# Rows of the first chunk transposed by a diagonal of inverse deviations, first-layer weights loaded and rounded by blocks

## What is computed

```
xn = layernorm(x)                      # (x - mean) / sqrt(var + 1e-5), per row of 256
D = fractal_dimension(xn)              # one scalar from the first 1024 numbers of xn
x1 = ifft(fft(xn) * wave_filter(D)).real
corrected = golay_correct(sigmoid(x1 @ W_el + b_el) > 0.5)    # 24 bits a token
attn = x1 + corrected @ W_le + b_le
ffn = gelu(xn @ w1 + b1) @ w2 + b2     # 256 -> 1024 -> 256
out = x + attn + ffn
```

## Time and profile before

| | |
|---|---|
| median of 3 runs | 407.12 us (407.1 to 407.69) |
| the profiled execution: its own time | 407.3 us |
| its span, first to last instruction | 405.5 us |
| PE busy | 400.7 us, 99% |
| DVE, ACT, POOL busy | 298.7 (74%), 223.3 (55%), 87.2 us (21%) |
| granted TensorE clock, mean | 1.000 |
| DMA | 35.75 MB, mean 88 GB/s |

### The profile page before, as it was taken

How to read it: one execution, slowest core, us unless ns; L and a number is a source line. 1 busy time by engine, 2 the same in 40 slices (tenths; PEclk the granted TensorE clock), 3 DMA queues, 4 the chain that set the end, 5 groups by cost and what they waited for, 6 DMA issues and landing times.

```text
span 405.5 us, 5548 instructions
## 1 busy us (share of the span) xinstructions
PE 400.7 (99%) x1774; PEld 329.1 (81%) x1774; DVE 298.7 (74%) x512; ACT 223.3 (55%) x333; POOL 87.2 (21%) x102
## 2 busy tenths in 40 slices
PE   8999999999999999999999999999999999999997
PEld 3888888888888888888888888888888888888886
DVE  5879985878658795677957788476974868757656
ACT  3967556557354664537545474554736556365561
POOL 3142421313003131121313013131121312113000
PEclk9999999999999999999999999999999999999999
DMA  6554333213333213333123332023333031111011
GB/s 187 218 158 156 104 103 106 63 42 104 103 104 98 44 65 103 104 103 97 46 64 104 103 104 90 26 91 103 104 103 78 40 89 53 54 52 52 2 52 52
DMA packets 15307, 35.75 MB, mean 88 GB/s; under 512 B 5440, under 2 KB 6592, under 8 KB 15296
## 3 DMA queue, kind: packets, MB, share of 16 engines
q1 hardware_dynamic: 15152, 35.49, 27.4%
q10 hardware_dynamic: 144, 0.13, 0.1%
HBM read 27.17 MB, written 8.45 MB: 88 GB/s over the span
## 4 chain that ended last, share of the span: by engine, by line
PE 97%; DMA 1%; DVE 1%; POOL 0%; SPq 0%; issue 0%
PE p_h L964 43%; PE p_f L982 28%; PE p_f L987 14%; PE p_s L1030 5%; PE p_l L1017 4%; PE p_s L1038 2%; DMA x_sb<-x 1%; PE p_f L997 0%; SPq L248 0%; DVE stats L830 0%; POOL row_nums L361 0%; DVE rows_sb L817 0%; PE p_g L1006 0%; PE p_l L1006 0%; PE p_s L1139 0%
## 5 line engine op out<-in xcount | busy, mean ns | idle before, releaser
L446 ACT ACTIVATE h<-p_h,small_sb 128x512 f32<-128x512 f32 x128 | 88.2, 689 | 139.4 <-PE p_h L964 138.9
L633 DVE TENSOR_TENSOR h_lo<-h,h_hi 128x512 fp32r<-128x512 f32 x128 | 102.9, 804 | 69.2 <-ACT h_hi L454 69.2
L982 PE MATMUL p_f<-h_hi,w_hi 128*128 128x512 f32 x252 | 98.3, 390 | 0.0
L982 PE MATMUL p_f<-h_hi,w_lo 128*128 128x512 f32 x252 | 98.1, 389 | 0.0
L369 POOL TENSOR_TENSOR uv<-xn 128x512 f32<-128x512 f32 x30 | 59.3, 1996 | 126.0 <-DVE xn L618 126.0
L454 ACT CAST h_hi<-h 128x512 fp32r<-128x512 f32 x128 | 79.5, 621 | 5.8
L964 PE MATMUL p_h<-xT_hi,w_hi 128*128 128x512 f32 (+1 forms) x258 | 79.4, 389 | 0.0
L964 PE MATMUL p_h<-xT_lo,w_hi 128*128 128x512 f32 (+1 forms) x258 | 79.2, 388 | 0.0
L964 PE MATMUL p_h<-xT_hi,w_lo 128*128 128x512 f32 (+1 forms) x258 | 79.0, 387 | 0.0
L987 PE MATMUL p_f<-h_lo,w_hi 128*128 128x512 f32 x252 | 77.6, 389 | 0.0
L964 PEld LDWEIGHTS p_h<-xT_lo,w_hi 128*128 128x128 f32 x258 | 48.3, 188 | 10.3 <-DVE xT_lo L839 0.2
(11 more groups left out here) (127 smaller groups left out, 325.2 us busy)
## 6 DMA issues: line engine op xcount, KB each, us to landing
xt_sb<-xt SPq DMA_DIRECT2D x16, 512.0 KB, 5.3
x_sb<-x SPq DMA_DIRECT2D x15, 512.0 KB, 4.6
rows_sb<-rows_dram SPq DMA_DIRECT2D x15, 512.0 KB, 4.4
out<-xt_sb SPq DMA_DIRECT2D x15, 512.0 KB, 2.8
xt_sb<-w SPq DMA_DIRECT2D x3, 512.0 KB, 7.5
xt_sb<-w SPq DMA_DIRECT2D x2, 256.0 KB, 4.5
x_sb<-x SPq DMA_DIRECT2D x2, 128.0 KB, 2.1
x_sb<-x SPq DMA_DIRECT2D x1, 256.0 KB, 3.2
```

Of the source, the lines that this page charges most:

```text
L446: nc.scalar.activation(h[m % 2][:], p_h[:, m % 2, :], ACT.Gelu, bias=small_sb[:, S_B1 + m:S_B1 + m + 1]).then_inc(gelu_done, 1)
L633: nc.vector.tensor_tensor(h_lo[m % HR][:], h[m % 2][:], h_hi[m % HR][:].bitcast(F32), ALU.subtract).then_inc(h_lo_done, 1)
L982: mm(p_f[:, a, :], w[:, m, a * HF:(a + 1) * HF], h_hi[r][:], start=(m == 0 and w is w2_hi), stop=False, skip_group_check=True)
```

## The change

- The identity is no longer loaded: POOL makes it with `affine_select` from the tile of ones, ahead of four memsets.
- DVE only centres chunk 0's rows (`centre_rows`), half 0 between the two statistics, and waits for no power. ACT multiplies the identity by each tile's inverse deviations (`deviations`), and PE multiplies the centred rows by that diagonal with plain fp32 matrix products (`turn_rows`) where it transposed before.
- w1's first load and first part are cut in two blocks; the small inputs are issued ahead of them, and chunk 1 of x ahead of w2's first half.
- On ACT the first transposed half is cast ahead of the first weights, and the second half's diagonals and cast are interleaved with weight blocks 0 and 1. On DVE the low parts alternate in the same way, and chunk 1's statistics go ahead of the first hidden low part.
- On PE blocks 0 and 1 of `up` are both made in halves of 256 columns, in an order written out in `first_ups`; there are 10 products on zeros instead of 12; the last sum of the fractal dimension goes behind `down` of block 2 instead of block 1.

```diff
@@ -20,8 +20,8 @@
 BANK = 512
-W1_PARTS = ((0, 2), (2, 4), (4, 6), (6, MB))
-W1_LOADS = ((0, 2), (2, 4), (4, MB))
+W1_PARTS = ((0, 1), (1, 2), (2, 4), (4, 6), (6, MB))
+W1_LOADS = ((0, 1), (1, 2), (2, 4), (4, MB))
 W2_PARTS = ((0, 2), (2, 4), (4, MB))
@@ -31,7 +31,7 @@
 SEG = 32
-IDLE = 12
+IDLE = 10
 HALF = CT // 2
@@ -89,6 +89,8 @@
         uv = sb("uv", [P, KB, CTOK], F32)
+        by_dev = uv[:, :, :].rearrange("p a (j t) -> p (a j) t", t=P)[:, 0:CT, :]
         xT_hi = [sb(f"xT_hi{i}", [P, KB, CTOK], F32R) for i in range(2)]
@@ -296,14 +298,14 @@
                              rows_dram[par].rearrange("a t -> (a t)").partition_broadcast(P)).then_inc(rows_in[par], 16)
-            sp.dma_start(id_sb[:], ident).then_inc(id_in, 16)
+            sp.dma_start(small_sb[:], small).then_inc(small_in, 16)
             load_w1(0)
-            sp.dma_start(small_sb[:], small).then_inc(small_in, 16)
             load_w1(1)
+            load_w1(2)
             sp.dma_start(con[:], consts).then_inc(con_in, 16)
+            load_x(1)
             load_w2(0)
-            load_x(1)
-            load_w1(2)
+            load_w1(3)
             load_w2(1)
@@ -337,10 +339,13 @@
             nc.gpsimd.memset(ones[:], 1.0).then_inc(pool_set, 1)
+            pool.wait_ge(pool_set, 3)
+            nc.gpsimd.affine_select(out=id_sb[:], in_=ones[:], pattern=[[1, P]], base=0, channel_multiplier=-1,
+                                    compare_op=ALU.is_equal, fill=0.0).then_inc(id_made, 1)
             for q in range(2):
...
                 nc.gpsimd.memset(le2[q][:].bitcast(F32), 0.0).then_inc(le_set, 1)
-            pool.wait_ge(pool_set, 3)
             links = [0]
@@ -512,22 +517,36 @@
                 nc.scalar.copy(w2_hi[:, m0:m1, :], w2_f[:, m0:m1, :]).then_inc(w2_hi_ready, 1)
-            w1_part_hi(0)
-            for g in range(2):
+            def deviations(g):
+                act.wait_ge(rstd_done, g + 1)
+                for j in range(g * HALF, (g + 1) * HALF):
+                    last = nc.scalar.mul(by_dev[:, j, :], id_sb[:], row_nums[0][:, 1, j:j + 1])
+                last.then_inc(dev_made, 1)
+            def turned_rows_hi(g):
                 act.wait_ge(t0_done, g + 1)
                 nc.scalar.copy(half_tokens(xT_hi[0], g), half_bank(g)).then_inc(t0_hi, 1)
+            act.wait_ge(id_made, 1)
+            deviations(0)
+            turned_rows_hi(0)
+            w1_part_hi(0)
+            deviations(1)
             w1_part_hi(1)
+            turned_rows_hi(1)
+            w1_part_hi(2)
             act.wait_ge(small_in, 16)
...
             hidden_hi(0, 0, first=True)
+            gelu(0, 1, first=True)
             w2_part_hi(0)
-            gelu(0, 1, first=True)
             hidden_hi(0, 1, first=True)
-            w1_part_hi(2)
+            w1_part_hi(3)
             gelu(0, 2, first=True)
...
             w2_part_hi(1)
-            w1_part_hi(3)
+            w1_part_hi(4)
             gelu(0, 3, first=True)
@@ -810,14 +829,12 @@
                                         ALU.subtract).then_inc(w2_ready, 1)
-            def normalise(g):
-                dve.wait_ge(rstd_done, g + 1)
+            def centre_rows(g):
+                dve.wait_ge(stat_done, g + 1)
                 for j in range(g * HALF, (g + 1) * HALF):
-                    last = nc.vector.tensor_scalar(xn0[:, j, :], x_sb[0][:, j, :], mv[0][:, j, 0:1],
-                                                   row_nums[0][:, 1, j:j + 1], ALU.subtract, ALU.mult)
+                    last = nc.vector.tensor_scalar(xn0[:, j, :], x_sb[0][:, j, :], mv[0][:, j, 0:1], None, ALU.subtract)
                 last.then_inc(xn0_done, 1)
@@ -825,19 +842,19 @@
             aggregate(0, range(HALF))
+            centre_rows(0)
             dve.wait_ge(x_in[0], 16)
...
             aggregate(0, range(HALF, CT))
-            for g in range(2):
-                normalise(g)
-            w1_part_lo(0)
+            centre_rows(1)
             for g in range(2):
...
                                         ALU.subtract).then_inc(t0_lo, 1)
+                w1_part_lo(g)
             table = [P, NS, FRE]
@@ -853,6 +870,9 @@
             nc.vector.tensor_reduce(fr_s[:, 0, :], fr_a[:], AX.X, ALU.add).then_inc(part_sums, 1)
+            statistics(1, 1)
+            dve.wait_ge(stats_made, 3)
+            aggregate(1)
             hidden_lo(0, 0)
@@ -860,11 +880,8 @@
             nc.vector.tensor_reduce(fr_s[:, 2, :], fr_a[:], AX.X, ALU.add).then_inc(part_counts, 1)
-            w1_part_lo(2)
+            w1_part_lo(3)
             hidden_lo(0, 1)
-            statistics(1, 1)
-            dve.wait_ge(stats_made, 3)
-            aggregate(1)
             hidden_lo(0, 2)
@@ -872,7 +889,7 @@
                                     ALU.add).then_inc(logged, 1)
-            w1_part_lo(3)
+            w1_part_lo(4)
             w2_part_lo(1)
@@ -944,27 +961,60 @@
                     if first and m == m0:
-                        pe.wait_ge(*((w1_hi_ready, 1) if n == 0 else (w1_ready, n + 1)))
-                if not (first and m < 2):
-                    pe.wait_ge(gelu_done, MB * c + m - 1)
-                groups = 2 if first and m == 0 else 1
-                for g in range(groups):
-                    tok = slice(g * CTOK // groups, (g + 1) * CTOK // groups)
-                    n = 0
-                    for w, xp in ((w1_hi, xT_hi), (w1_lo, xT_hi), (w1_hi, xT_lo)):
-                        if groups == 2:
-                            if w is w1_lo and g == 0:
-                                pe.wait_ge(w1_ready, 1)
-                            elif w is w1_hi:
-                                pe.wait_ge(t0_hi if xp is xT_hi else t0_lo, g + 1)
-                        for k in range(KB):
-                            last = mm(p_h[:, m % 2, tok], w[:, k, m * P:(m + 1) * P], xp[par][:, k, tok],
-                                      start=(n == 0), stop=(n == 3 * KB - 1))
-                            n += 1
+                        pe.wait_ge(w1_ready, n + 1)
+                pe.wait_ge(gelu_done, MB * c + m - 1)
+                n = 0
+                for w, xp in ((w1_hi, xT_hi), (w1_lo, xT_hi), (w1_hi, xT_lo)):
+                    for k in range(KB):
+                        last = mm(p_h[:, m % 2, :], w[:, k, m * P:(m + 1) * P], xp[par][:, k, :],
+                                  start=(n == 0), stop=(n == 3 * KB - 1))
+                        n += 1
                 last.then_inc(up_done, 1)
+            def turn_rows(g):
+                pe.wait_ge(xn0_done, g + 1)
+                pe.wait_ge(dev_made, g + 1)
+                for k in range(KB):
+                    for j in range(HALF):
+                        last = mm(half_bank(g)[:, k, j * P:(j + 1) * P], xn0[:, g * HALF + j, k * P:(k + 1) * P],
+                                  by_dev[:, g * HALF + j, :], start=True, stop=True, skip_group_check=True)
+                last.then_inc(t0_done, 1)
+            def half_up(m, g, terms, last_term=2):
+                tok = slice(g * GTOK, (g + 1) * GTOK)
+                for n in terms:
+                    w, xp = ((w1_hi, xT_hi), (w1_lo, xT_hi), (w1_hi, xT_lo))[n]
+                    for k in range(KB):
+                        last = mm(p_h[:, m, tok], w[:, k, m * P:(m + 1) * P], xp[0][:, k, tok],
+                                  start=(n == 0 and k == 0), stop=(n == last_term and k == KB - 1), skip_group_check=True)
+                return last
+            def first_ups():
+                turn_rows(0)
+                pe.wait_ge(t0_hi, 1)
+                pe.wait_ge(w1_hi_ready, 1)
+                half_up(0, 0, (0,))
+                turn_rows(1)
+                pe.wait_ge(w1_hi_ready, 2)
+                half_up(1, 0, (0,))
+                pe.wait_ge(w1_ready, 1)
+                half_up(0, 0, (1,))
+                pe.wait_ge(t0_lo, 1)
+                half_up(0, 0, (2,))
+                half_up(1, 0, (2,), last_term=1)
+                pe.wait_ge(w1_ready, 2)
+                half_up(1, 0, (1,), last_term=1)
+                pe.wait_ge(t0_hi, 2)
+                half_up(0, 1, (0, 1))
+                half_up(1, 1, (0, 1))
+                pe.wait_ge(t0_lo, 2)
+                half_up(0, 1, (2,)).then_inc(up_done, 1)
+                half_up(1, 1, (2,)).then_inc(up_done, 1)
             def down(c, m, first=False):
@@ -1130,18 +1180,9 @@
                 mm(p_f[:, 0, :], idle[:, 0:P], idle[:], start=True, stop=True)
-            pe.wait_ge(id_in, 16)
-            for g in range(2):
-                pe.wait_ge(xn0_done, g + 1)
-                for k in range(KB):
-                    for j in range(HALF):
-                        last = nc.tensor.transpose(half_bank(g)[:, k, j * P:(j + 1) * P],
-                                                   xn0[:, g * HALF + j, k * P:(k + 1) * P], id_sb[:])
-                last.then_inc(t0_done, 1)
             pe.wait_ge(pool_set, 3)
-            for m in range(LOOK):
+            first_ups()
```

(3 more changed lines are left out.)

12 lines of the change are left out of this document (6 added, 6 removed).

## The result

The changed kernel takes 413.49 us (median of 5, 412.05 to 414.19) against 407.22 us (407.1 to 407.69, n = 5) of the kernel before: a ratio of 1.0147, interval [1.0127, 1.0168]. The prediction said slower, 410.0 us within 408.8 to 411.6. The direction is right and the size is not: 6.3 us came where 2.9 were forecast.

A forecast was written before the change was run, and what follows sets the result against it. The prediction took PE's unbroken stream as the bound (97% of the chain): the marker shifts by +2.7 us and 0.2 comes behind it, total +2.9, giving 410.0 us from a median of 407.12, range 408.8 to 411.6.

The forecast's parts named there:

- marker: Start on PE of the m=2 products of up: 11.68 us before, forecast at 14.36, a shift of +2.7 us.
- step 3: ACT casts half 0 and w1's first block before the second diagonals (8.14 to 8.83); its queue costs 1.1 us.
- Step 6: PE, after eight 256-column products, waits from 10.77 for w1's second low part, ready on DVE at 11.67.
- Step 8: Nothing covers gelu of m=0 (13.50 to 14.19), so the m=2 products wait and start at 14.36.
- step 2: PE turns half 0 from 5.91, ending at 7.31 with passes taking double until about 6.5.
- Behind the marker: After the start of m=2: moved dimension sum, POOL chain 5.21 long ending at 28.1, costing 0.2 us, between 0 and 1.
- part (b) of "Removed": In the head, two idle products fewer, 0.84 us, so that PE is free near 5.5 and not 6.3.
- step 1: ACT writes the first half's diagonals from 5.17 to 5.86, after the first power, ready at 5.13.
- The clock stays at 1.2 GHz into the products: Rival: in the head, turns and early 256-column products run slow, +1.5, about 411.5 us; chance 0.15.
- POOL late: Rival: in the head, affine_select takes over 2.15 us and delays both powers, about 411.2 us; chance 0.06.
- Faster: Rival: in the head, the earlier start carries through and m=2 starts up to 1 us earlier, about 406 us; chance 0.05.
- Four passes: Rival: each plain product in the turns takes four passes, both turns grow by 0.88, 411.8 us; chance 0.03.

The follow-up runs named there:

- a_idle14: The changed kernel with 14 idle products on zeros in place of 10: 412.43 us against 407.25 for the kernel before, ratio 1.0125.
- b_sum_late: The kernel before with only the last sum of the fractal dimension moved behind down of block 2: 408.89 us against 407.23, ratio 1.0041.
- a_sum_back: The changed kernel with the last sum of the fractal dimension put back behind down of block 1: 412.23 us against 407.29, ratio 1.0102.
- b_idle10: The kernel before with 10 idle products on zeros in place of 12: 408.1 us against 407.29, ratio 1.0022.
- a_transposed: The changed kernel with the diagonal undone, DVE scaling and PE transposing by the identity again: 410.89 us against 407.29, ratio 1.0084.
- a_idle18: The changed kernel with 18 idle products on zeros in place of 10: 412.77 us against 407.29, ratio 1.0126.
- a_dev_early: The changed kernel with 18 idle products, sum put back, both diagonals before ACT's first cast, both turns together on PE: 409.55 us against 407.27.

## Why the prediction was right in direction and wrong in size

The move of 6.2 us (413.49 less the 407.25 beside a_idle14) comes apart so:

| term | forecast | measured | by |
|---|---|---|---|
| marker, at the high clock | +2.7 | +3.0 | a_idle14 |
| wait for the basis behind it | +0.2 | +1.7 | a_idle14, b_sum_late |
| clock in the head, with what a late x costs | 0 | +1.1 | changed kernel less a_idle14 |
| outside the span (2.0 for 1.8) | 0 | +0.2 | a_idle14's profiled execution; 1.7 to 2.0 in its five |
| not assigned | | 0.2 | |

- **The steps of the sum to the marker were right, given its start.** Two passes a product: eight records a half, 1.05 us. The Trainium skill's rule (TensorE: Matmul & The Clock Gate, section Terms: 4 times faster for FP32) does not fit these rows, where a plain product has twice the records of a transpose, not four times. ACT's second diagonals behind w1's first block, step 3: so in the trace, and taking it away, with PE's turns put together, gave 1.7 us. Step 6, DVE's low part: 0.78 us of waiting. Step 8, the uncovered gelu: 0.69. The nearness of 3.0 to 2.7 is in part luck: in a_idle14 the first turn begins at 6.42 and not at 5.91, and takes 1.05 and not the 1.40 that step 2 gave it, so that two errors nearly cancel. The late start is made of small things: POOL's first add took 0.35 instead of 0.20; ACT to PE took 0.14 where I had 0.05; and fourteen idle products reach to 6.4, 0.2 past where PE is wanted.
- **Failed: "Behind the marker", the term taken as 0.2, between 0 and 1.** The delay in it was right: counted from the marker, POOL's chain begins 1.8 us later than before (27.87 - 16.78 against 20.99 - 11.68), and I had 1.9. What failed is "the POOL chain (5.21 long)". I moved a chain and kept its length, and its length depends on what DVE does beside it. Before, the chain was over at 26.20, and DVE's centring of chunk 1 began at 26.54, a row of the kernel before that the sum leaves out:

```profile
26.54 1.23 DVE L613 TENSOR_TENSOR xn<-xt_sb,rows_sb 128x1024 f32<-128x1024 f32 x1 [0.94 <-DMA rows_sb<-rows_dram]
```

A chain 1.8 us later must run into it, as the centring itself did not move: it starts at 31.67, and 31.67 less the marker's 5.1 is 26.57. Its excess here is 0.33 (0.53 for 0.20) + 0.86 + 0.49 (1.19 for 0.70) + 0.32 = 2.0 us. 1.8 + 2.0, less 1.2 of cover on ACT (26.20 to 27.50 before, 35.09 to 35.18 now) and 0.8 between scaling and product (27.50 to 28.78 before, 35.18 to 35.63 now), is 1.8, against the 1.7 of PE's wait.
- **Failed: part (b) of "Removed", two idle products at 0.84 us, "so that PE is free near 5.5".** I priced them at the low pace. In the changed kernel's profile the high level had come by 3.9 us, the last ones run at 0.22 a piece and the ten are over at 4.87. The moment of the rise differs between executions: the same ten were over at 5.42 in a_sum_back, and at 5.64 and 5.70 in b_idle10 and a_transposed, where it came later. Instead of meeting the diagonals they leave 2.05 us of nothing, and the clock fell back behind it. a_idle14 and a_idle18 show that this gap is what matters: with more idle products, and the same work behind them, no execution had a mean below 0.998.
- **Failed: the start of step 1, the first power "ready at 4.42 + 0.71 = 5.13".** I took it over from the kernel before. In the changed kernel's profile it is ready at 5.99: the second piece of x landed 0.72 later (4.03 for 3.31), and POOL's first add took 0.16 more. Of the gap of 2.05 us, where the sum had 0.4, 1.0 is that PE's first turn came at 6.93 instead of 5.91, and 0.6 that the idle products were over before 5.5. In a_sum_back's profile, with the same head, the idle products were over at 5.42, close to the 5.5 of the sum, and the clock still fell behind 1.74 us of nothing, since its power was ready only at 6.22. The rival *The clock stays at 1.2 GHz into the products* named a low clock, at +1.5 and with a chance of 0.15. What came is a fall after a rise, +1.1 on the median together with x's lateness, and 1.56 behind the first turn in the profile.
- **Failed: the range.** It took the slow clock and the stall behind the marker as alternatives and not as two things that can come together. 410.0 + 1.5 + 0.8 would have reached 412.3, still below the result.
- **Right at nothing:** `affine_select` (0.29 us, over long before 4.15), w2's later landing, DVE's moved statistics. The rivals POOL late, Faster, No difference and Four passes are each contradicted by a row shown above.
- **Open:** what makes the second piece of x land at 3.3 us in one execution and at 4.3 in another, and how much of the 6.2 us the new order of the loads takes by it; why an execution of the changed kernel took 413.98 with a granted mean of 1.000 (a late rise isn't seen in the mean, but without a trace of that execution this is only argued); and whether plain products keep the clock up better than transposes, which no pair of runs separates.

## What to carry to other kernels

When a change moves a chain of small operations in time, lay it over the other engines' rows at its new place before taking its length from the old one. Price work on an in-order queue by its place in it: the same diagonals cost 0.5 us ahead of the casts, and moving them there, with PE's turns, gave 1.7 us (a_dev_early). Count idle products that warm the clock so that they reach to the first real work even where the rise comes early and the last of them run at the fast pace: a gap behind them cost up to 3 us, and the two that were left out had cost 0.4 to 0.8. Take the start of the chain from the changed kernel's own loads, not from the old trace.

## What the runs showed of the hardware

- **POOL stands still beside some of DVE's operations.** Each slow POOL operation of the chain above ends 0.06 us behind the DVE operation beside which it started: 27.87 + 1.12 = 28.99 and 27.71 + 1.22 = 28.93; 31.89 + 1.06 = 32.95 and 31.67 + 1.22 = 32.89; 33.02 + 1.19 = 34.21 and 32.92 + 1.23 = 34.15; 34.29 + 0.52 = 34.81 and 34.07 + 0.68 = 34.75. So its length is what is left of DVE's, and one instruction of four elements a partition took 0.20, 0.70 or 1.19 us. It is a wait, not a lower speed. The Trainium skill (SBUF — State Buffer, section Who interferes with whom) states it as an exclusive lock between DVE operations with two inputs in SBUF and GpSimd; these traces agree, with 0.06 us as the way out of it. I had not used that rule.
- **Not settled:** POOL's first `var_eps` took 0.36 us where it was 0.20. It stands beside DVE's first centring operation, which has one tensor input, and ends in the same way 0.06 behind it: 4.82 + 0.36 = 5.18 and 4.77 + 0.35 = 5.12. The second `var_eps`, at 6.41 in the same trace, stands beside such an operation too and took 0.20; there the DVE operation took 0.38 instead of 0.35.
- **TensorE's clock fell back after it had risen.** In the changed kernel the rise in the idle products at 3.9 us did not hold over 2 us in which PE had nothing, and the record then shows 0.50 from 8.7 to 14.2 us while PE was busy 4.49 of those 5.50 us. Granted means below 0.998 came in 11 of 24 executions with ten idle products and in none with twelve or more.
- **A load's landing varies:** the second piece of x, issued at the same place, landed by 3.31 to 3.62 us in six profiles with the old loads behind it and by 3.30 to 4.26 in eleven with the new ones, and the head starts with it.
